# First layer of a two-layer attention kernel: softmax denominators from an all-ones matmul, inverted in eight pieces, and a new split of the norm blocks

## What is computed

```python
x = x + L0_xattn(layernorm(x), ctx, mask, Wq, Wk, Wv, Wo)     # 16 heads, 8 kv heads, head width 128
x = x + L0_ffn(layernorm(x), factors, bias)                   # sum of 8 factors, one linear map
x = x + L1_xattn(layernorm(x), ctx, Wq, Wk, Wv, Wo, gq, gk)   # rmsnorm on q and k
x = x + L1_ffn(layernorm(x), w_router, we1, we3, we2, ws1, ws3, ws2)  # 16 experts, top 4, and a shared one

# L0_xattn, per batch and head
scores = q @ k.T / sqrt(128); attn = softmax(scores); out = (attn @ v) @ Wo
# L1_xattn needs rsqrt(mean(k * k) + 1e-5) of every key and head, with k = ctx @ Wk
```

## Time and profile before

| what | value |
|---|---|
| median of three executions | 2184.47 us |
| profiled execution | 2184.68 us |
| its span, first to last instruction | 2182.9 us |
| PE busy | 2129.5 us (98%) |
| PE weight loads busy | 1565.0 us (72%) |
| DVE (VectorE) busy | 1566.5 us (72%) |
| ACT (ScalarE) busy | 951.6 us (44%) |
| POOL (GpSimd) busy | 1350.9 us (62%) |
| mean granted TensorE clock | 0.996 |

### The profile page before, as it was taken

The page is one execution under the profiler, slowest core; times in us unless marked ns, Lnnn a source line. Parts: engine busy times, 40 slices in busy tenths (PEclk is TensorE's granted clock), DMA queues, the critical chain, the costliest instruction groups (busy, mean ns, idle before and its releaser), DMA issues. The chain is left out here.

```text
span 2182.9 us, 27103 instructions
## 1 busy us (share of the span) xinstructions
PE 2129.5 (98%) x8898; PEld 1565.0 (72%) x8898; DVE 1566.5 (72%) x2574; ACT 951.6 (44%) x2536; POOL 1350.9 (62%) x1056
## 2 busy tenths in 40 slices
PE   7999999999999999999999999899999999999999
PEld 6777777777777777777777655566666666665998
DVE  4689888988898888988896433656666666652577
ACT  3454454444444455444445225444444343431432
POOL 0378777877687767877787300088778787771221
PEclk9999999999999999999999999999999999999999
DMA  3000000000000000000001410011110111101110
GB/s 131 15 29 15 29 29 15 15 29 29 15 15 29 29 15 25 19 29 15 29 11 39 145 40 0 21 50 49 37 57 29 57 44 42 43 1 51 37 52 25
DMA packets 15134, 75.62 MB, mean 35 GB/s; under 512 B 1746, under 2 KB 2114, under 8 KB 13986
## 3 DMA queue, kind: packets, MB, share of 16 engines
q1 hardware_dynamic: 14994, 73.89, 10.4%
HBM read 72.97 MB, written 0.92 MB: 34 GB/s over the span
## 5 line engine op out<-in xcount | busy, mean ns | idle before, releaser
L618 POOL TENSOR_TENSOR l_prod<-l_prod 125x256 f32<-125x256 f32 x576 | 417.2, 738 | 270.6 <-DVE l_prod L683 270.0
L683 DVE TENSOR_TENSOR l_prod<-l_side,xq 125x512 f32<-125x512 f32 x576 | 394.5, 685 | 55.7 <-PE l_side L814 48.8
L959 POOL TENSOR_TENSOR l_acc<-l_acc,l_probs 125x896 f32<-125x896 f32 x160 | 346.0, 2163 | 81.4 <-ACT l_probs L909 65.6
L559 ACT ACTIVATE l_probs<-l_slots,mask_bias 125x448 f32<-125x448 f32 x384 | 238.1, 632 | 343.0 <-PE l_slots L753 342.9
L979 DVE TENSOR_TENSOR l_scaled<-l_slots,rk 125x896 f32<-125x896 f32 x192 | 207.0, 1084 | 197.8 <-PE l_slots L1044 197.6
L612 POOL TENSOR_TENSOR l_acc<-l_acc,l_probs 125x896 f32<-125x896 f32 x160 | 338.5, 2116 | 0.0
L541 ACT ACTIVATE l_prod_act<-l_prod_act 125x128 f32<-125x128 f32 x768 | 228.0, 298 | 235.5 <-DVE l_prod_act L683 235.4
L909 ACT ACTIVATE l_probs<-l_scaled 125x896 f32<-125x896 f32 x192 | 182.8, 952 | 320.7 <-DVE l_scaled L979 295.7
L692 DVE TENSOR_REDUCE l_msq<-l_prod 125x4 f32<-125x256 f32 x576 | 234.6, 410 | 1.6
L646 DVE SCALAR_TENSOR_TENSOR top<-l_side,mask_bias,top 125x448 f32<-125x448 f32 x330 | 223.1, 676 | 6.7 <-PE l_side L797 5.8
L1042 PE MATMUL l_slots<-l_qhi,l_clo 128*125 128x448 f32 x384 | 203.0, 529 | 1.4 <-DVE l_qlo L984 1.4
(11 more groups left out here) (241 smaller groups left out, 4374.6 us busy)
## 6 DMA issues: line engine op xcount, KB each, us to landing
land<-in_ctxT SPq DMA_DIRECT2D x32, 750.0 KB, 4.4
l_nat<-in_ctxN SPq DMA_DIRECT2D x16, 750.0 KB
post_we<-in_experts SPq DMA_DIRECT2D x20, 384.0 KB, 3.0
spare<-in_ctxN SPq DMA_DIRECT2D x8, 750.0 KB
nat<-in_ctxN SPq DMA_DIRECT2D x8, 750.0 KB
spare<-in_wo SPq DMA_DIRECT2D x2, 2048.0 KB, 7.8
spare<-in_wqT SPq DMA_DIRECT2D x4, 512.0 KB, 4.3
mid_fac<-in_factors SPq DMA_DIRECT2D x1, 2048.0 KB, 8.0
```

The source lines that it names most:

```text
L559: act.activation(P[t % NP][:, HALF * i:HALF * i + HALF], bank_of("S", t, i)[0:KT, 0:HALF], ACT.Exp, bias=m.mask_bias[:, b, t:t + 1]).then_ ...
L618: pool.tensor_tensor(buf[:, :, 0:C // 2], buf[:, :, 0:C // 2], buf[:, :, C // 2:C], ALU.add).then_inc(s.half_sum, 1)
L683: dve.tensor_tensor(to[:, :, :], bank, xt.unsqueeze(1).to_broadcast([KT, 4, C]), ALU.mult).then_inc(s.side_dve, 1)
L959: pool.tensor_tensor(acc[:, :], acc[:, :], P[t % NP][:, :], ALU.add).then_inc(s.acc, 1)
```

## The change

Four things, all in the first layer's attention, plus the removal of the buffer `inv`:

1. `sums` is two f32 matmuls a batch with all-ones weights, one for each half of 448 columns. Each gives the sums of its columns on all 128 partitions. `spread` and its eight matmuls are gone. `ORDER` has D for half 0, D for half 1 and an unused place where D, E, E were.
2. ScalarE copies the two banks into a new buffer `den` (128x896) at the start of step 1 (`sums_out`), and TensorE's bank wait is on that copy (`den_out`).
3. VectorE inverts `den` in place in eight pieces of 128x112, one after the fourth side job of each of the steps 2 to 9; GpSimd multiplies the outputs by them, half 0 in step 7 and half 1 in step 11. After the last batch the eight pieces and the two multiplies stand at the end.
4. Norm blocks: a tile gives two or three N blocks and two or one A blocks in turn, 30 N and 18 A a batch instead of 36 and 12. In steps 2, 3, 4, 6, 7 and 9 one N of the list becomes an A. N has four product buffers instead of five.

```diff
-NPROD, NPROD_ACT, LAG_N, NLOW = 5, 2, 3, 4
-NBLK = NT * DVE_G
+NPROD, NPROD_ACT, LAG_N, NLOW = 4, 2, 3, 4
+BLOCKS_N = [(t, g) for t in range(NT) for g in range(3 - t % 2)]
+BLOCKS_A = [(t, g) for t in range(NT) for g in range(3 - t % 2, NG)]
+NBLK, NBLK_A = len(BLOCKS_N), len(BLOCKS_A)
...
-STEPS = ["MNMNM", "MNAMNMN", "NMNAMNNM", "NMANMNM", "NMNAMNNM", "NMNAMNM", "ANMNNMN", "NNMANMN", "NAMNNMA", "NTANTNN", "ANNA", ""]
+STEPS = ["MNMNM", "MNAMNMN", "NMNAMNAM", "NMANMAM", "NMNAMNAM", "NMNAMNM", "ANMNAMN", "NAMNAMN", "NAMNNMA", "NTANTNA", "ANNA", ""]
...
-ORDER = [("S", 0, 0), ("S", 0, 1), ("S", 1, 0), ("S", 1, 1), ("D", 0, 0), ("E", 0, 0), ("E", 0, 1)]
+ORDER = [("S", 0, 0), ("S", 0, 1), ("S", 1, 0), ("S", 1, 1), ("D", 0, 0), ("D", 0, 1), ("-", 0, 0)]
...
+        den = sb("den", [C, 2, HALF], F32)
...
                 if kind == "D" and b > 0:
-                    return pe.wait_ge(s.inv, b)
-                if kind == "E" and b > 0:
-                    return pe.wait_ge(s.o_done, 2 * b - 1 + half)
+                    return pe.wait_ge(s.den_out, 2 * b - 1 + half)
...
+            def sums_out(b):
+
+                for half in range(2):
+                    act.wait_ge(s.den, 2 * b + half + 1)
+                    need(act, s.o_done, 2 * b)
+                    act.activation(den[:, half, :], bank_of("D", 0, half)[:, 0:HALF], ACT.Copy).then_inc(s.den_out, 1)
...
                 for t in range(NT):
+                    if t == 1 and b > 0:
+                        sums_out(b - 1)
...
+            def normalise(b, half):
+
+                pool.wait_ge(s.o_raw, b + 1)
+                pool.wait_ge(s.inv, QBLK * b + 4 * half + 4)
+                o = m.qs[:, b, :, :].rearrange("p (a h) q -> p a (h q)", a=2)[:, half, :]
+                pool.tensor_tensor(o, o, den[:, half, :], ALU.mult).then_inc(s.o_done, 1)
...
+                    if b > 0 and t in (7, 11):
+                        normalise(b - 1, t // 11)
...
+            def invert(b, j):
+
+                dve.wait_ge(s.den_out, 2 * b + j // 4 + 1)
+                part = den[:, j // 4, TT * (j % 4):TT * (j % 4) + TT]
+                dve.reciprocal(part, part).then_inc(s.inv, 1)
...
-                        invert(b - 1)
                         twice_less_high(b)
-                    if t == 1 and b > 0:
-                        normalise(b - 1)
-                    for n in jobs:
+                    for at, n in enumerate(jobs):
                         side_job(n)
+                        if at == 3 and b > 0 and 2 <= t < 2 + QBLK:
+                            invert(b - 1, t - 2)
...
             def sums(b):
 
                 pe.wait_ge(s.acc, (NT - 1) * (b + 1))
-                wait_bank(pe, b + 1, "D", 0, 0)
...
+                for half in range(2):
+                    wait_bank(pe, b + 1, "D", 0, half)
+                    pe.matmul(bank_of("D", 0, half)[:, 0:HALF], m.ones[0:KT, :], acc[:, HALF * half:HALF * half + HALF],
+                              start=True, stop=True).then_inc(s.den, 1)
...
-            def spread(b):
...
-                    if t == 1 and b > 0:
-                        spread(b - 1)
```

More of the change, by code:

```diff
@@ L58, in plan @@
                 STEP_JOBS[b, t].append(add("V", b))
-    assert all(made[kind, b] == (n if kind in "NA" or b > 0 else 0) for b in range(B) for kind, n in zip("MTNA", (2 * NT, 2, NBLK, NT)))
+    assert all(made[kind, b] == (n if kind in "NA" or b > 0 else 0) for b in range(B) for kind, n in zip("MTNA", (2 * NT, 2, NBLK, NBLK_A)))
 plan()
@@ L439, in first_attention @@
         "ld_land", "ld_nat0", "ld_nat1", "ctx_hi", "ctx_lo", "q_hi", "q_lo", "nat_hi", "xq", "shift",
-        "scores", "probs", "pv", "acc", "den", "inv", "spread", "o_raw", "o_done",
+        "scores", "probs", "pv", "acc", "den", "den_out", "inv", "o_raw", "o_done",
         "ld_wv", "ld_wo", "side_pe", "side_dve", "side_act", "half_sum", "sum_dve", "sum_act", "rk_pre"])
@@ L533, in add_up @@
             def add_up(n):
-                b, t, at = JOBS[n].b, JOBS[n].i, number(n, "A") - 1
+                b, (t, g), at = JOBS[n].b, BLOCKS_A[JOBS[n].i], number(n, "A") - 1
                 act.wait_ge(s.side_dve, number(n, "MTNA"))
-                if t == 0:
+                if JOBS[n].i == 0:
                     need(act, s.rk_pre, b)
@@ L540, in add_up @@
                     whole = prod_act[at % NPROD_ACT][:, c, :]
-                    last = act.activation(whole, whole, ACT.Copy, accum_out=msq[:, t, 12 + c:13 + c])
+                    last = act.activation(whole, whole, ACT.Copy, accum_out=msq[:, t, 4 * g + c:4 * g + c + 1])
                 last.then_inc(s.sum_act, 1)
@@ L586, in _ @@
                     nat_high(b + 1)
+            sums_out(B - 1)
         @block.gpsimd
@@ L606, in add @@
                 if t == 1:
-                    need(pool, s.den, b)
+                    need(pool, s.den, 2 * b)
                     pool.tensor_tensor(acc[:, :], P[0][:, :], P[1][:, :], ALU.add).then_inc(s.acc, 1)
@@ L631, in _ @@
                             halve(n)
+            for half in range(2):
+                normalise(B - 1, half)
         @block.vector
@@ L675, in multiply @@
                     need(dve, s.sum_dve, at + 1 - NPROD)
[L676 removed]
+                    to, (t, g) = prod[at % NPROD], BLOCKS_N[i]
                 else:
                     need(dve, s.sum_act, at + 1 - NPROD_ACT)
[L679 removed]
+                    to, (t, g) = prod_act[at % NPROD_ACT], BLOCKS_A[i]
                 dve.wait_ge(s.side_pe, n + 1)
@@ L686, in add_up @@
             def add_up(b, i):
-                t, g, at = i // DVE_G, i % DVE_G, NBLK * b + i
+                (t, g), at = BLOCKS_N[i], NBLK * b + i
                 if i == 0:
@@ L704, in side_job @@
                         add_up(JOBS[n].b, JOBS[n].i - LAG_N)
-            def invert(b):
-                dve.wait_ge(s.den, b + 1)
-                dve.reciprocal(m.inv[0:QBLK, :], bank_of("D", 0, 0)[0:QBLK, 0:TT]).then_inc(s.inv, 1)
-            def normalise(b):
-                dve.wait_ge(s.o_raw, b + 1)
-                o = m.qs[:, b, :, :].rearrange("p (a h) q -> p a (h q)", a=2)
-                for half in range(2):
-                    dve.wait_ge(s.spread, 2 * b + half + 1)
-                    dve.tensor_tensor(o[:, half, :], bank_of("E", 0, half)[:, 0:HALF], o[:, half, :],
-                                      ALU.mult).then_inc(s.o_done, 1)
             for b in range(B):
@@ L726, in _ @@
                             jobs = jobs[1:]
-                        invert(b - 1)
                         twice_less_high(b)
-                    if t == 1 and b > 0:
-                        normalise(b - 1)
-                    for n in jobs:
+                    for at, n in enumerate(jobs):
                         side_job(n)
+                        if at == 3 and b > 0 and 2 <= t < 2 + QBLK:
+                            invert(b - 1, t - 2)
+                    if b == B - 1 and 2 <= t < 2 + QBLK and len(jobs) < 4:
+                        invert(b - 1, t - 2)
                     if t == NT - 1:
@@ L735, in _ @@
                             add_up(b, i)
-            invert(B - 1)
-            normalise(B - 1)
+            for j in range(QBLK):
+                invert(B - 1, j)
         @block.tensor
@@ L768, in sums @@
                 pe.wait_ge(s.acc, (NT - 1) * (b + 1))
-                wait_bank(pe, b + 1, "D", 0, 0)
-                out = bank_of("D", 0, 0)
-                for j in range(QBLK):
-                    last = pe.matmul(out[:, 0:TT], m.row_of[0:KT, 127 - j:255 - j], acc[:, TT * j:TT * j + TT],
-                                     start=j == 0, stop=j == QBLK - 1)
-                last.then_inc(s.den, 1)
-            def spread(b):
-                pe.wait_ge(s.inv, b + 1)
-                for half in range(2):
-                    wait_bank(pe, b + 1, "E", 0, half)
-                    out = bank_of("E", 0, half)
-                    for j in range(4):
-                        last = pe.matmul(out[:, TT * j:TT * j + TT], m.ident[:, 4 * half + j:4 * half + j + 1].to_broadcast([128, 128]), m.inv[:, :],
-                                         start=True, stop=True)
-                    last.then_inc(s.spread, 1)
+                for half in range(2):
+                    wait_bank(pe, b + 1, "D", 0, half)
+                    pe.matmul(bank_of("D", 0, half)[:, 0:HALF], m.ones[0:KT, :], acc[:, HALF * half:HALF * half + HALF],
+                              start=True, stop=True).then_inc(s.den, 1)
             def side_job(n):
@@ L810, in side_job @@
                 else:
-                    t, g = (i // DVE_G, i % DVE_G) if kind == "N" else (i, DVE_G)
+                    t, g = (BLOCKS_N if kind == "N" else BLOCKS_A)[i]
                     keys, cols = slice(KT * t, KT * t + KT), slice(512 * g, 512 * g + 512)
@@ L840, in _ @@
             sums(B - 1)
-            spread(B - 1)
 def second_attention(nc, m, a, tag, sem):
```

9 lines of the change are left out of this document (2 added, 7 removed).

## The result

The changed kernel took 2199.93 us (median of four, 2197.99 to 2200.67), the kernel before 2184.28 in the same session: ratio 1.0071, 95% interval 1.0056 to 1.0085. That is +15.65 us, where +35.5 was forecast. The direction was right, the size was not.

A forecast was written before the change was run, and what follows sets the result against it. TensorE was taken as the bound, with VectorE close behind: 36.8 (VectorE) − 7.0 (boundaries) + 3.65 (end) + 2 (clock) = +35.5 us on 2184.7, predicted 2220, range 2184 to 2233 (forecast's own 2193 to 2230).

The forecast's parts named there:

- The bank wait of the second ones-matmul: Batch boundary: TensorE waits about 2 us for ScalarE's exponential of (b, 1, 0), so the gain is 1.0 us, not 2.07.
- Rival B: Boundary: VectorE's slack swallows the pieces and the bank wait does not bind either; 2159 us, chance 0.05.
- VectorE decides: Steps 2 to 9: the pieces make VectorE late in freeing side banks, so TensorE waits; +36.8 us in all.
- Rival A: Steps 2 to 9: VectorE's slack swallows the pieces, making the kernel faster; 2175 us, chance 0.13.
- VectorE's term: Steps 2 to 9, batches 1 to 14: late VectorE shifts TensorE by 2.63 us a batch, +36.8 us.
- The price of a piece: VectorE, steps 2 to 9: each 128x112 reciprocal costs 0.78 us start to start, eight +6.2 us a batch.
- the ledger: Steps 2 to 9: lateness carried through 58 VectorE jobs, each against TensorE's third job after it; shift 2.63 us.
- The buffer waits: VectorE, four product buffers: a norm block directly after another waits a guessed 0.1 us, twice, +0.2 us a batch.
- The ScalarE chain: Step 9 to the boundary: last norm block ends 0.57 us later, cutting the boundary gain from 1.0 to 0.43.
- Rival C: Boundary: ScalarE's queue becomes the bound, its chain delayed by a whole 1.19 us; 2229 us, chance 0.14.
- The end: After the last batch: copy, eight pieces and GpSimd's second multiply delay the next stage by 3.65 us.
- The clock behind it: After the layer's end: TensorE's idle stretch of some 8 us lowers its granted clock, +2 us (0 to 4).

The follow-up runs named there:

- experiment 1: Changed kernel without the reciprocals of the denominators, GpSimd multiplying by the sums themselves: 2172.68 us, batch 70.42.
- experiment 13: Changed kernel with pieces of 128 instead of 112 columns, overlapping by 16, each waiting for the one before: 2215.42 us, batch 72.87.
- experiments 5 to 7 and 14: Kernel before plus reciprocals a batch: eight 128x112, four 128x112, eight 128x56 (four product buffers), eight 128x112 (five buffers): 2231.64, 2205.76, 2203.29, 2220.71 us.
- experiment 9: Changed kernel with the pieces at the boundary and the second ones-matmul behind both value sums of step 0: 2167.62 us.
- experiment 3: Changed kernel with the old division of norm blocks (36 N, 12 A) and the old order of steps: 2224.71 us, batch 73.72.
- experiment 11: Changed kernel with the last batch alone bringing out its denominators as before the change: 2195.22 us.
- experiment 10: Changed kernel with nine more f32 matmuls of 448 columns on TensorE behind the layer's last sums: 2198.81 us.
- experiments 12 and 9: 12: changed kernel with pieces at the boundary, second ones-matmul behind both value sums, last batch ended as before: 2163.59 us. 9: without that old end, 2167.62 us.

## Why the prediction was right in its mechanism and wrong in its size

- **The bank wait of the second ones-matmul**: right. 1.73 us before it by the exponential of (b, 1, 0) (some 2 forecast), boundary gain 0.96 (1.0 forecast). Only entering the last batch, which was counted like the others, it is 1.00. Rival B falls.
- **VectorE decides**: right. It is what turns a gain of 0.85 us a batch (experiment 1) into a loss of 0.85. Rival A falls.
- **VectorE's term, 2.63 us a batch by step 11**: this is the step that failed; the term was mis-sized. From the scores of step 1 on and against the kernel before (medians of eleven batches), TensorE's scores end 0.26 us late in step 4, 0.95 in steps 5 and 6, 1.09 in step 8, and 1.50 in step 11. The 1.13 too many have two parts. (a) The price of a piece. The prediction read 0.78 from start to start and did not look one instruction further; the net price is 0.69, 0.75 us a batch less, and at the rate of experiment 13 about 0.71 of it reaches TensorE. This is most of the error. Experiment 13, where a piece costs what the prediction took, bears it out: there the scores of step 11 end 2.27 us late, 0.77 more than in the changed kernel. (b) What is left, some 0.4, is slack that the ledger did not count: it carried every lateness to the third job as if each value sum and score between them started at once. That this is the reason is argued, not shown. The buffer waits, guessed as two of 0.1 us, were right: two of 0.11 in steps 2 to 9 (a third in step 10). My other picture, that slack takes the first pieces whole and only the later ones cost, is not borne out either: slack goes by degrees (experiments 5 to 7 and 14).
- **The ScalarE chain, 0.57 us late**: it was 0.29 (0.77 against 0.48). It came late because VectorE gave out the blocks late; with the pieces at the boundary it is gone (0.48 again, experiment 9), and with the old split, where VectorE is later still, the boundary is 0.53 later (experiment 3). Rival C, the chain a whole 1.19 us late, falls.
- **The end**: 3.43 us measured, 3.65 forecast. **The clock behind it**: 3.0, forecast 2 (0 to 4).
- **Not forecast**: a second slow stretch in the last stage, +1.4, and the scatter of start and batch 0, -2.8 between these two profiles. Neither belongs to the change: the slow stretch is in nine of the sixteen profiles, among them two doses with the old denominators, and missing in three kernels with the new ones.

In sum: the fifteen batches behind batch 0 are 11.0 us longer between the two spans, where 29.8 was forecast (36.8 − 7.0). With the end −0.2, the clock behind it +1.0, the slow stretch of the last stage +1.4 and the start −2.8 this makes 35.5 − 18.8 − 0.2 + 1.0 + 1.4 − 2.8 = 16.1, where the spans differ by 16.0. For a batch in the middle 2.63 − 0.43 = 2.20 was forecast and 0.85 came; of the 1.35 between them VectorE's term is 1.13 and the ScalarE chain 0.28.

The time lies inside the forecast's own range of 2193 to 2230, near its low end. That end stood for VectorE's idle time being used whole, 0.7 us a batch, which is not what happened; the start's −2.8, which is luck, brought the time further down.

Of the Trainium skill's rule that SBUF sources have 62 cycles less fixed time than PSUM ones ("VectorE: DVE Perf Modes", the TRN2 errata): the 128x112 reciprocal from SBUF lasts 841 ns, the 8x112 one from PSUM 0.85 us. The 65 ns are not there: where rule and measurement differ, the measurement decides. What made the pieces cheaper is mainly the shorter step behind them (0.07 us on average; start to start they take 0.76 instead of 0.78).

## What to carry to other kernels

Price an added instruction by two distances, its start to the next start and that one's to the one after, in a trace where the same neighbours stand. An engine that hands banks to the bottleneck passes on nearly every further microsecond once its slack is used up (0.75 of 0.79), less before (1.44 of some 3.5), and none in a place where it waits for others: the same eight reciprocals cost 1.70 us a batch in steps 2 to 9 and nothing at the boundary. Look at the last boundary by itself: no casts stand in its chain, and there the new place did cost a wait (0.97 us). A relief is worth nothing until something uses the cover up: the same six blocks were worth 0 and 1.60 us a batch.

## What the runs showed of the hardware that I had not expected

- A reciprocal of 56, 112 and 128 columns lasts 492, 842 and 942 ns, 6.25 ns a column and 0.14 us fixed, but the next instruction starts after 0.41, 0.76 and 0.86 us and itself gives way 0.05 to 0.09 us sooner. Small ones lose almost nothing by being small.
- TensorE idled 7.67 us at the end of the layer and was then granted 0.50 for 4 us and 0.74 for the next 4; with the old end, where the idle time comes in two pieces of about 1 us (experiment 11), it kept 1.00, and with work of no use in the gap (experiment 10) too. A wait of 2.07 us before the last batch was followed by 4 us at 0.57 in one kernel and by full clock in another (experiments 12 and 9).
- In the last stage, behind 32 router matmuls of 16 columns, the clock falls in some profiles and not in others, which costs 1.3 to 3.1 us (from the first of them to the end 147.1 to 147.3 us without it, 148.5 to 150.2 with it). The kernel after, then the kernel before, in the 6 us behind those matmuls:

```profile
2053.40:2059.40 6.00, 6.00 (x24) 5.46 (x24) 1.50 (x4) 3.04 (x5) 0.00 (x0) 0.72 0.00 0
```

```profile
2038.70:2044.70 6.00, 6.00 (x31) 5.48 (x31) 2.22 (x5) 3.88 (x6) 0.77 (x1) 1.00 0.00 0
```
